# A two-layer sequence kernel on one core: output product and slot values in three rounded products of high and low parts

## Chip, cores and metric

One core of a Trainium2 chip. The metric is the device time of one execution in microseconds (us); lower is better. TensorE is called PE in rows, its weight loads PEld; VectorE is DVE, ScalarE ACT, GpSimd POOL.

## What is computed

Input x is 32 sequences of 512 tokens of 256 numbers, all float32. Two layers follow one another, each on a normalized x and added to x.

```
# layer 1, per sequence: attention by a kernel of random features
q     = tanh(x @ W_charge.T + b_charge)                  # one number per token
shell = normalize(x @ W_shell.T + b_shell)
phi   = (powers of q  (x)  [cos, sin](shell @ omega.T + rff_bias)) @ W_combine.T
attn  = softmax(causal(phi @ phi.T * decay / temp))
out   = (attn @ (x @ W_v.T + b_v)) @ W_out.T + b_out
# layer 2, per sequence: 64 slots, 8 chosen per token
h     = gelu([x, mean slot] @ w1.T + b1);  logits = (h @ w2.T + b2) / (|tau| + 0.1)
alpha = softmax over the 8 largest logits, 0 elsewhere   # tokens x 64
gi    = alpha.T @ x / sum of alpha                       # 64 x 256
S_new = gru(gi, slots)                                   # 64 x 256
slot_values = S_new @ wv.T + bv
out   = (alpha @ slot_values) @ wo.T + bo
```

The kernel folds wo into wv, so the last two lines are slot_values = S_new @ Wvo + bSV and out = alpha @ slot_values.

## The kernel before

The 32 sequences are worked in 16 pairs k = 0..15; d = 0, 1 is the sequence in the pair, b = 2k + d. Every engine has a queue written out by hand (an order of calls such as `values(n, 1); xm_t(f, 1, 0)`), with semaphores between them. The queue of each engine has an opening (pairs 0 to 4, to about 185 us), a loop `for it in range(3, 15)` that works on five pairs at once, and an end. In the loop p = it + 2 is the pair being normalized and projected, n = it + 1 the one in attention, f = it the one at the second layer's hidden product and routing, m = it - 1 the one in the GRU, g = it - 2 the one at its output. There are 8 banks of PSUM in three rings (T for transposes, L for logits, G for the rest); a step that takes a bank waits until the step that emptied its last user is done.

The steps that matter, by engine:
- TensorE: `xn_t` transposes the normalized x (line 332), `proj` multiplies it with high and low parts of the weights (349), `q_t`, `z_t` transpose the features, `phi` (392 to 398), `logits` (415), `e_t`, `values` (443), `xm_t`, `hidden` (476), `route` (488), `rt_t`, `gather` (511), `gi_t`, `gx_rz` and `gx_n` (526), `al_t` transposes alpha, `slot_v` (597) makes the slot values, `out_mm(k, u)` (621) the output of token blocks 2u and 2u + 1 of both sequences: sequence d lies in rows 64d to 64d + 63 of aT and SV.
- ScalarE: `ln_norm` (746) normalizes x with the scales of GpSimd, `xn_high` (756), `v_high` (768 to 771), `z_copy` (801) copies the feature transpose that the powers start from, `al_copy` (896), activations.
- VectorE: statistics, the low parts (`xn_low` 988, `v_low` 995, `probs_low` 1052, `xm_low` 1090), `row_max` (1044), `attended` (1068), `top` (1106, 1109), `chosen` (1134), `gathered` (1147), `gates`, `candidate`, `new_slots` (1182), `slot_values` (1190, adds the bias), `finish` (1199, adds the output to x).
- GpSimd: `ln_scale` (eight small operations that end at 1485), `lm_scale`, `lm_norm` (268), `slot_change` (294), `rnorm`, `phase`, `power(p, i)` (241: four products 512 wide, the first waits for z_copy), `shift8` (277), `alpha` (287).

Most large products are made as three float32r products of high and low parts: ScalarE rounds the operand to float32r (the high part), VectorE subtracts it from the original (the low part), and TensorE adds high x high, high x low and low x high. `slot_v` and `out_mm` are plain float32 products, which TensorE runs as two instructions each.

The loop of GpSimd before:

```python
for it in range(3, 15):
    p, f, m = it + 2, it, it - 1
    ln_scale(p, 0); ln_scale(p, 1); lm_scale(f, 0); lm_scale(f, 1); lm_norm(f, 0); lm_norm(f, 1)
    slot_change(m); rnorm(p); phase(p); power(p, 0); shift8(f, 0); power(p, 1); power(p, 2)
    shift8(f, 1); alpha(f, 0); power(p, 3); alpha(f, 1)
```

## Time and profile before

| | |
|---|---|
| median of 3 runs | 692.98 us (691.63 to 694.11) |
| profiled execution, its time | 692.77 us |
| its span, first to last instruction | 691.0 us |
| busy: PE, DVE, ACT, POOL | 97%, 88%, 74%, 56% |
| granted clock of TensorE, mean | 0.998 of full speed |

Busy time is the time in which an engine has an instruction in flight. Matmuls overlap, so a busy PE may still stand between two starts; the starts in the timeline show that. A group of instructions is given by its line, its output and inputs and its shape.

### The profile page before, as it was taken

The page shows a single profiled execution, that of the slowest core. Times are in us where ns is not written, and L with a number is a line of the kernel's source. Part 1 is how long each engine was busy: PE and PEld are TensorE (multiplying, and loading weights), DVE is VectorE, ACT ScalarE, POOL GpSimd, SP SyncE. Part 2 cuts the span into 40 slices and gives each one's busy share as a digit, 9 for nine tenths or more (in the row PEclk, how much of TensorE's full clock was granted, in tenths as well). Part 3 has the DMA queues.
Part 4 walks back from the last instruction along what each step waited for, and adds up shares of the span by engine and source line. Part 5 has one row for each costly group of instructions (what it writes and reads, how often), then busy time and mean ns, then how long its engine had stood idle before and what let it go on. Part 6 is the DMA issues. An engine that isn't in the chain of part 4 may idle for free.

```text
span 691.0 us, 15834 instructions
## 1 busy us (share of the span) xinstructions
PE 672.0 (97%) x4622; PEld 541.1 (78%) x4622; DVE 604.9 (88%) x2001; ACT 514.7 (74%) x1477; POOL 384.9 (56%) x818
## 2 busy tenths in 40 slices
...
GB/s 237 108 153 83 10 63 1 63 2 137 48 121 64 40 144 3 129 56 123 62 64 122 1 139 46 123 62 88 98 1 158 28 123 62 63 62 63 1 2 182
DMA packets 49115, 54.11 MB, mean 78 GB/s; under 512 B 6212, under 2 KB 40582, under 8 KB 49030
## 3 DMA queue, kind: packets, MB, share of 16 engines
...
q8 instruction: 38, 0.62, 0.4%
...
## 4 chain that ended last, share of the span: by engine, by line
PE 83%; issue 4%; DVE 3%; POOL 3%; SPq 3%; ACT 2%; DMA 1%; POOLq 0%; DVEq 0%; ACTq 0%
PE ps L321 17%; PE ps L349 16%; PE ps L443 15%; PE ps L476 6%; PE ps L415 6%; PE ps L526 6%; PE ps L511 4%; PE ps L621 4%; PE ps L488 2%; SPq L1635 2%; PE ps L392 2%; PE ps L398 2%; PE ps L597 2%; PE ps L395 2%; POOL xm L268 1%
## 5 line engine op out<-in xcount | busy, mean ns | idle before, releaser
L241 POOL TENSOR_TENSOR Z<-Z,QB 128x512 f32<-128x512 f32 x60 | 77.3, 1288 | 81.5 <-ACT Z L801 79.8
L746 ACT ACTIVATE xn<-X,rs 128x255 f32<-128x255 f32 x128 | 66.4, 599 | 72.0 <-POOL rs L1485 72.0
L443 PE MATMUL ps<-Vh,Eh 128*128 128x256 f32 x320 | 88.5, 304 | 0.1
L349 PE MATMUL ps<-W1h,xh 128*128 128x354 f32 x256 | 88.5, 346 | 0.0
L349 PE MATMUL ps<-W1h,xl 128*128 128x354 f32 x256 | 83.2, 325 | 0.6 <-DVE xl L988 0.5
L349 PE MATMUL ps<-W1l,xh 128*128 128x354 f32 x256 | 83.0, 324 | 0.0
L443 PE MATMUL ps<-Vl,Eh 128*128 128x256 f32 x320 | 80.8, 280 | 0.0
L995 DVE TENSOR_TENSOR Vl<-ps,Vh 128x256 fp32r<-128x256 f32 x128 | 53.5, 420 | 22.7 <-ACT Vh L771 20.2
L1052 DVE TENSOR_TENSOR El<-ps,Eh 128x128 fp32r<-128x128 f32 (+3 forms) x128 | 61.7, 483 | 13.3 <-ACT Eh L822 11.7
L812 ACT ACTIVATE E<-ps,nmax 128x128 f32<-128x128 f32 (+3 forms) x128 | 67.9, 536 | 5.2 <-DVE nmax L1044 4.9
L268 POOL TENSOR_SCALAR xm<-X,rs 128x256 f32<-128x256 f32 x120 | 67.6, 579 | 1.5 <-PE ps L511 0.8
L822 ACT ACTIVATE Eh<-ps 128x128 fp32r<-128x128 f32 (+3 forms) x128 | 55.4, 444 | 11.6 <-PE ps L321 9.2
L443 PEld LDWEIGHTS ps<-Vh,Eh 128*128 128x128 f32 x320 | 60.3, 188 | 4.5 <-DVE X L1068 3.0
L1044 DVE CUSTOM_DVE_ANT_0 ps<-ps,causal 128x128 f32<-128x128 f32 (+3 forms) x128 | 60.9, 498 | 2.7 <-PE ps L415 2.6
L443 PEld LDWEIGHTS ps<-Vl,Eh 128*128 128x128 f32 x320 | 60.4, 189 | 0.1
L1068 DVE SCALAR_TENSOR_TENSOR X<-ps,rinv,X 128x256 f32<-128x256 f32 x128 | 59.3, 474 | 1.1 <-PE ps L443 0.6
L443 PE MATMUL ps<-Vh,El 128*128 128x256 f32 x320 | 58.6, 280 | 0.7 <-DVE El L1052 0.7
L321 PE MATMUL ps<-ident,E 128*128 128x128 f32 x320 | 55.2, 278 | 0.9 <-DVE El L1052 0.4
L1079 DVE BATCH_NORM_STATS2 stats<-X 128x6 f32<-128x256 f32 x128 | 51.7, 415 | 0.0
L321 PEld LDWEIGHTS ps<-ident,E 128*128 128x128 f32 x320 | 36.4, 140 | 19.3 <-issue 13.2
L771 ACT ACTIVATE Vh<-ps 128x256 fp32r<-128x256 f32 x128 | 51.4, 401 | 0.0
L1090 DVE TENSOR_TENSOR xmL<-ps,xmT 128x512 fp32r<-128x512 f32 x62 | 42.4, 686 | 10.1 <-ACT xmT L833 9.6
...
## 6 DMA issues: line engine op xcount, KB each, us to landing
...
```

The source lines that it names most:

```text
L241: e.tensor_tensor(Z[:, i + 1, :], Z[:, i, :], QB[:, :], ALU.mult).then_inc(s["zm"], 1)
L268: ins = e.tensor_scalar(xm[:, b % 3, t, 0:D], X[:, b % NX, t, :], rs2[:, d, 2, t:t + 1], rs2[:, d, 1, t:t + 1], ALU.add, ALU.mult)
L321: ins = e.transpose(p[0:m, j * 128:j * 128 + 128], block_in, ident[:, :])
L349: ins = e.matmul(p[:, 0:FEATS], x[:, d, c, t * 128:t * 128 + 128], w[:, c, :], start=j == 0, stop=j == 5)
L443: ins = e.matmul(p[:, 0:D], w[:, r % 2, j * 128:j * 128 + 128], v[:, (2 * k + d) % 4, j, :], start=z == 0, stop=z == len(parts) - 1)
L746: ins = e.activation(xn[:, d, t, 0:D - 1], X[:, b % NX, t, 0:D - 1], ACT.Identity, bias=rs[:, d, 2, t:t + 1], scale=rs[:, d, 1, t:t + 1])
L812: e.activation(E[:, r % 3, 0:w], at["lg", r], ACT.Exp, bias=nmax[:, r % 8:r % 8 + 1], scale=-1.0, accum_out=rsum[:, r % 8:r % 8 + 1]).then ...
L822: e.activation(Eh[:, r % 2, 0:w], at["E", r][:, 0:w], ACT.Copy).then_inc(s["eh"], 1)
L995: e.tensor_tensor(Vl[:, b % 4, t, :], at["vs", b, t][:, 0:D], Vh[:, b % 4, t, :].bitcast(FP), ALU.subtract).then_inc(s["vl"], 1)
L1044: e.tensor_tensor_reduce(at["lg", r], at["lg", r], causal[:, N - w:N], 1.0, 3e38, ALU.add, ALU.min, nmax[:, r % 8:r % 8 + 1]).then_inc(s[" ...
L1052: e.tensor_tensor(El[:, r % 2, 0:w], at["E", r][:, 0:w], Eh[:, r % 2, 0:w].bitcast(FP), ALU.subtract).then_inc(s["ET"], 1)
L1068: e.scalar_tensor_tensor(X[:, b % NX, i, :], at["av", r][:, 0:D], rinv[:, r % 8:r % 8 + 1], X[:, b % NX, i, :], ALU.mult, ALU.add).then_in ...
```

## The change

`slot_v` and `out_mm` become three rounded products of high and low parts. `out_mm` stays as it was for pairs 0 and 15 (`EXACT`). ScalarE makes the high parts (`sn_high`, `sv_high`, `al_high`), GpSimd the low parts (`sn_low`, `sv_low`, `al_low`). The new parts lie in buffers of the first layer: those of the slots and of the slot values in xh, that of alpha in xl, alpha's transpose in hT; GIN and GI move into gt and gn. So steps that write those buffers get waits. The order of all four compute queues is new. Wvo is stored as Wvh and Wvl by two more VectorE operations in the setup. The core of the diff:

```diff
+        GIN = gt[:, :, :, :].rearrange("p c b s -> p (c b s)")
+        GI = gn
+        SNh = xh[:, 0, 0, 0:D].rearrange("p (c b s) -> p c b s", c=2, b=2)
+        SNl = xh[:, 0, 0, D:2 * D].rearrange("p (c b s) -> p c b s", c=2, b=2)
+        SVh = xh[:, 1, 1, 0:D]
+        SVl = xh[:, 1, 1, D:2 * D]
+        aTl = xl[:, 1, 1, :]
+        aTx = hT[:, 1, :]
+        EXACT = (0, NP - 1)
+        def projected(k, d):
+            return 8 * min(k + (3 if k else 4), NP - 1) + 4 * d + 4
 # slot_v
-                for c in range(2):
-                    if c == 0 and k == NP - 1:
-                        e.wait_ge(s["sh"], 1)
-                    else:
-                        e.wait_ge(s["sn"], k + 1)
-                    ins = e.matmul(p[:, 0:D], SN[:, c, :, :].rearrange("p b s -> p (b s)"), Wvo[:, c, :],
-                                   start=c == 0, stop=c == 1)
+                e.wait_ge(s["snh"], k + 1)
+                parts = [(SNh, w, c) for c in range(2) for w in (Wvh, Wvl)] + [(SNl, Wvh, c) for c in range(2)]
+                for j, (x, w, c) in enumerate(parts):
+                    if j == 4:
+                        e.wait_ge(s["snl"], k + 1)
+                    ins = e.matmul(p[:, 0:D], x[:, c, :, :].rearrange("p b s -> p (b s)"), w[:, c, :],
+                                   start=j == 0, stop=j == 5)
 # out_mm
-                    e.wait_ge(s["aT"], k + 1)
-                    e.wait_ge(s["sv"], k + 1)
+                    e.wait_ge(s["aT" if exact else "ath"], k + 1 if exact else k)
+                    e.wait_ge(s["sv" if exact else "svh"], k + 1 if exact else k)
+                parts = [(aTx, SV)] if exact else [(aT, SVh), (aTl, SVh), (aT, SVl)]
                 for t in range(2):
                     tok = slice((2 * u + t) * 128, (2 * u + t) * 128 + 128)
-                    for d in range(2):
+                    for j, (w, v) in enumerate(parts):
+                        if u == 0 and t == 0 and j:
+                            e.wait_ge(s["atl" if j == 1 else "svl"], k)
+                        for d in range(2):
...
+                            ins = e.matmul(p[:, t * D:t * D + D], w[own(d), tok], v[own(d), :],
+                                           start=j == 0 and not final, stop=j == len(parts) - 1,
+                                           skip_group_check=True)
 # ScalarE: waits of xn_high and gelu, new steps
+                if k >= 5 and c == d:
+                    e.wait_ge(s["of_mm"] if c else s["sv_mm"], 4 * (k - 4) + 4 if c else k - 3)
+                if k >= 3 and d == 1:
+                    e.wait_ge(s["atl"], k - 2)
+            def al_high(k):
...
+                e.wait_ge(s["aT"], k + 1)
+                if k > 1:
+                    e.wait_ge(s["of_mm"], 4 * k)
+                e.activation(aT[:, :], aTx, ACT.Copy).then_inc(s["ath"], 1)
+            def sn_high(k):
+                e.wait_ge(s["vs_mm"], projected(k, 0))
+                if k < NP - 1:
+                    e.wait_ge(s["sn"], k + 1)
+                    e.activation(SNh, SN[:, :, :, :], ACT.Copy).then_inc(s["snh"], 1)
...
+            def sv_high(k):
...
+                e.wait_ge(s["sv"], k + 1)
+                e.wait_ge(s["vs_mm"], projected(k, 1))
+                e.wait_ge(s["of_mm"], 4 * k)
+                e.activation(SVh, SV[:, :], ACT.Copy).then_inc(s["svh"], 1)
 # VectorE: new_slots waits for snl in place of sv_mm; gathered for sn; xn_low(p, 1, 1) for out_mm
-                    e.wait_ge(s["sv_mm"], k)
+                    e.wait_ge(s["snl"], k)
+            def end_low_setup():
+                e.wait_ge(s["snh"], NP)
+                e.tensor_tensor(SNl, SN[:, :, :, :], SNh.bitcast(FP), ALU.subtract).then_inc(s["snl"], 1)
 # GpSimd
+            def sn_low(k):
+                e.wait_ge(s["snh"], k + 1)
+                e.tensor_tensor(SNl, SN[:, :, :, :], SNh.bitcast(FP), ALU.subtract).then_inc(s["snl"], 1)
+            def al_low(k):
...
+                e.wait_ge(s["ath"], k)
+                e.wait_ge(s["vs_mm"], projected(k, 1))
...
+                e.tensor_tensor(aTl, aTx, aT[:, :].bitcast(FP), ALU.subtract).then_inc(s["atl"], 1)
+            def sv_low(k):
...
+                e.wait_ge(s["svh"], k)
+                e.tensor_tensor(SVl, SV[:, :], SVh.bitcast(FP), ALU.subtract).then_inc(s["svl"], 1)
```

The loops of TensorE (its changed lines), ScalarE and GpSimd:

```diff
 # TensorE
-                proj(p, 0, 2); e_t(n, 1); gx_n(m); xn_t(p, 1, 1); values(n, 0); proj(p, 0, 3); logits(n, 1)
-                out_mm(g, 1); xm_t(f, 0, 0); xm_t(f, 0, 1); e_t(n, 2); proj(p, 1, 0); proj(p, 1, 1)
+                xn_t(p, 1, 1); out_mm(g, 1); logits(n, 1); gx_n(m); e_t(n, 1); values(n, 0); proj(p, 0, 2)
+                proj(p, 0, 3); xm_t(f, 0, 0); proj(p, 1, 0); proj(p, 1, 1); xm_t(f, 0, 1); e_t(n, 2)
...
-                values(n, 3); z_t(p); rt_t(f); values(n, 4); values(n, 5); al_t(m); e_t(n, 6); slot_v(m)
+                values(n, 3); z_t(p); rt_t(f); values(n, 4); values(n, 5); slot_v(m); e_t(n, 6); al_t(m)
                 e_t(n, 7); values(n, 6); values(n, 7); phi(p); gather(f); logits(p, 0); out_mm(m, 0); gi_t(f)
 # ScalarE
+                sv_high(g); ln_norm(p, 0); gi_copy(m); xn_high(p, 0, 0); xn_high(p, 0, 1); expo(n, 0)
+                ln_norm(p, 1); v_high(p, 0, 0); expo(n, 1); expo(n, 2); expo(n, 3); v_high(p, 0, 1)
+                rz_tanh(m); probs_t(n, 0); xn_high(p, 1, 0); xn_high(p, 1, 1); v_high(p, 0, 2); probs_t(n, 1)
...
+                xm_copy(f, 1, 0); gelu(f, 0); xm_copy(f, 1, 1); sn_high(m); probs_t(n, 3); charge(p)
+                probs_t(n, 4); gelu(f, 1); sine(p); q_copy(p); rt_out(f); probs_t(n, 5); z_copy(p); expo(n, 6)
+                expo(n, 7); route_exp(f, 0); probs_t(n, 6); al_copy(m); probs_t(n, 7); route_exp(f, 1)
+                al_high(m)
 # GpSimd
+                ln_scale(p, 0); sv_low(g); ln_scale(p, 1); lm_scale(f, 0); lm_scale(f, 1); lm_norm(f, 0)
+                lm_norm(f, 1); slot_change(m); rnorm(p); phase(p); power(p, 0); sn_low(m); shift8(f, 0)
+                power(p, 1); power(p, 2); shift8(f, 1); power(p, 3); alpha(f, 0); al_low(m); alpha(f, 1)
```

In the opening, VectorE had `top(2, 0, 0); top(2, 0, 1); top(2, 1, 0); top(2, 1, 1); shift(2, 0); probs_low(3, 5); shift(2, 1); new_slots(1); attended(3, 3)`; now it has `top(2, 0, 0); top(2, 0, 1); attended(3, 3); shift(2, 0); new_slots(1)`. In the end the last pair's variance and normalization (`end_scale_a_setup`, `end_norm_a_setup`) stand earlier on VectorE, and `sn_high(15)` and `end_low_setup` come between the last slots and `slot_v(15)`.

## Rows read from the trace of the kernel before

**Rows 1.** The page, parts 1 and 4: busy time, and the chain by engine.

```profile
PE 672.0 (97%) x4622; PEld 541.1 (78%) x4622; DVE 604.9 (88%) x2001; ACT 514.7 (74%) x1477; POOL 384.9 (56%) x818
PE 83%; issue 4%; DVE 3%; POOL 3%; SPq 3%; ACT 2%; DMA 1%; POOLq 0%; DVEq 0%; ACTq 0%
```

**Rows 2.** Busy time by stage: stretch, us, then PE, PEld, DVE, ACT, POOL, clock, DMA.

```profile
60.00:185.00 125.00, 121.10 (x834) 96.35 (x833) 108.34 (x354) 98.45 (x275) 76.77 (x150) 1.00 0.22 56
305.70:345.50 39.80, 39.79 (x282) 32.64 (x282) 36.42 (x121) 31.27 (x91) 24.39 (x51) 1.00 0.29 80
...
650.00:691.00 41.00, 32.12 (x216) 23.87 (x214) 29.07 (x104) 12.99 (x25) 3.38 (x4) 0.97 0.24 78
```

**Rows 3.** Timeline of ScalarE, 300 to 345: start, us, what, [idle before, released by].

```profile
303.48 2.07 ACT L746 ACTIVATE xn<-X,rs 128x255 f32<-128x255 f32 x4 [5.87 <-POOL rs L1485]
...
331.15 0.59 ACT L801 ACTIVATE Z<-ps 128x512 f32<-128x512 f32 x1
...
343.32 2.07 ACT L746 ACTIVATE xn<-X,rs 128x255 f32<-128x255 f32 x4 [5.86 <-POOL rs L1485]
```

**Rows 4.** Timeline of PE, 304.2 to 306.7, the seam of a pass.

```profile
304.28 1.03 PE L621 MATMUL ps<-SV,aT 64*128 64x256 f32 x8
305.24 0.44 PE L321 MATMUL ps<-ident,GIN 128*128 128x128 f32 x2
305.70 1.06 PE L321 MATMUL ps<-ident,xn 128*128 128x128 f32 x8
306.60 0.28 PE L526 MATMUL ps<-GI,wih 128*128 128x128 f32 x1
```

**Rows 5.** Waits, whole kernel: us in total, times, longest.

```profile
ACT xn L746 <- POOL rs L1485: 72.0, 13, 8.0
```

**Rows 6.** Starts inside 304.275 to 304.290 (matmuls, loads) and 304.49 to 304.51 (loads).

```profile
304.28 0.38 PE L621 MATMUL ps<-SV,aT 64*128 64x256 f32 x2
304.28 0.19 PEld L621 LDWEIGHTS ps<-SV,aT 64*128 64x128 f32 x2
304.50 0.19 PEld L621 LDWEIGHTS ps<-SV,aT 64*128 64x128 f32 x2
```

**Rows 7.** Timeline of PE, 331.5 to 339.1: slot_v, and rounded matmuls of values.

```profile
334.44 1.03 PE L597 MATMUL ps<-Wvo,SN 128*128 128x256 f32 x4
335.31 0.60 PE L321 MATMUL ps<-ident,E 128*128 128x128 f32 x4
...
337.42 0.28 PE L443 MATMUL ps<-Vh,Eh 128*128 128x256 f32 x1
...
338.36 0.62 PE L443 MATMUL ps<-Vh,El 128*128 128x256 f32 x4
```

**Rows 8.** The page, part 5: a rounding copy of 256 columns.

```profile
L771 ACT ACTIVATE Vh<-ps 128x256 fp32r<-128x256 f32 x128 | 51.4, 401 | 0.0
```

**Rows 9.** Groups of instructions of POOL by shape: busy, mean ns | idle before.

```profile
L241 POOL TENSOR_TENSOR Z<-Z,QB 128x512 f32<-128x512 f32 x60 | 77.3, 1288 | 81.5 <-ACT Z L801 79.8
...
L287 POOL TENSOR_TENSOR AL<-lg,asum 128x256 f32<-128x256 f32 x30 | 18.4, 614 | 25.6 <-DVE asum L1127 10.4 <-issue 9.1 <-DVE lg L1134 6.2
...
L294 POOL TENSOR_TENSOR gt<-S,gn 128x256 f32<-128x256 f32 x15 | 11.0, 734 | 22.1 <-ACT gn L877 22.1
```

**Rows 10.** Timeline of POOL, 300 to 345, from the first power on.

```profile
331.82 1.29 POOL L241 TENSOR_TENSOR Z<-Z,QB 128x512 f32<-128x512 f32 x1 [6.07 <-ACT Z L801]
...
336.93 0.61 POOL L287 TENSOR_TENSOR AL<-lg,asum 128x256 f32<-128x256 f32 x1 [0.83 <-issue]
337.50 1.30 POOL L241 TENSOR_TENSOR Z<-Z,QB 128x512 f32<-128x512 f32 x1
339.55 0.61 POOL L287 TENSOR_TENSOR AL<-lg,asum 128x256 f32<-128x256 f32 x1 [0.76 <-DVE asum L1127]
```

**Rows 11.** Timeline of the end: PE's last slot_v, and DVE's slot_values.

```profile
682.58 1.03 PE L597 MATMUL ps<-Wvo,SN 128*128 128x256 f32 x4
683.64 0.42 DVE L1190 TENSOR_TENSOR SV<-ps,bSV 128x256 f32<-128x256 f32 x1 [0.19 <-PE ps L597]
```

**Rows 12.** Waits of PE in the opening, 60 to 185.

```profile
PE ps L597 <- DVE X L1068: 1.5, 1, 1.5
```

More of the change, by code:

```diff
@@ L168, in build @@
         SV = sb("SV", [128, D])
-        aT = sb("aT", [128, N])
+        aT = sb("aT", [128, N], FR)
         def stacked(d, j):
@@ L705, in _ @@
-            values(2, 4); hidden(1, 1); e_t(2, 5); z_t(3); logits(2, 2); route(1); gx_n(0); values(2, 5)
-            al_t(0); e_t(2, 6); rt_t(1); proj(4, 0, 0); values(2, 6); phi(3); xn_t(4, 1, 0); e_t(2, 7)
-            proj(4, 0, 1); proj(4, 0, 2); logits(3, 0); xn_t(4, 1, 1); values(2, 7); proj(4, 0, 3)
-            proj(4, 1, 0); e_t(3, 0); proj(4, 1, 1); proj(4, 1, 2); xm_t(2, 0, 0); e_t(3, 1); proj(4, 1, 3)
-            slot_v(0); values(3, 0); xm_t(2, 0, 1); logits(3, 1); out_mm(0, 0); e_t(3, 2); hidden(2, 0)
@@ L710, in _ @@
-            gather(1); out_mm(0, 1); e_t(3, 3); values(3, 1); gi_t(1); values(3, 2); xm_t(2, 1, 0)
-            xm_t(2, 1, 1); e_t(3, 4); gx_rz(1); q_t(4); hidden(2, 1); z_t(4); logits(3, 2); route(2); gx_n(1)
-            rt_t(2); values(3, 3); e_t(3, 5); al_t(1); values(3, 4); values(3, 5); e_t(3, 6); e_t(3, 7)
-            slot_v(1); values(3, 6); values(3, 7); phi(4); gather(2); logits(4, 0); out_mm(1, 0); gi_t(2)
+            proj(0, 0, 0); proj(0, 0, 1); xn_t(0, 1, 0); proj(0, 0, 2); proj(0, 0, 3); xn_t(0, 1, 1)
@@ new lines, in _ @@
+            proj(3, 1, 1); xm_t(1, 0, 1); e_t(2, 1); proj(3, 1, 2); proj(3, 1, 3); logits(2, 1); e_t(2, 2)
+            xn_t(4, 0, 0); values(2, 0); gather(0); logits(2, 2); q_t(3); e_t(2, 3); values(2, 1)
+            values(2, 2); hidden(1, 0); gi_t(0); xm_t(1, 1, 0); xm_t(1, 1, 1); values(2, 3); hidden(1, 1)
+            z_t(3); e_t(2, 4); xn_t(4, 0, 1); gx_rz(0); values(2, 4); e_t(2, 5); route(1); e_t(2, 6)
+            values(2, 5); al_t(0); rt_t(1); e_t(2, 7); values(2, 6); proj(4, 0, 0); phi(3); gx_n(0)
@@ new lines, in _ @@
+            proj(4, 0, 1); logits(3, 0); xn_t(4, 1, 0); proj(4, 0, 2); xn_t(4, 1, 1); proj(4, 0, 3)
+            values(2, 7); e_t(3, 0); proj(4, 1, 0); xm_t(2, 0, 0); e_t(3, 1); proj(4, 1, 1); proj(4, 1, 2)
+            xm_t(2, 0, 1); proj(4, 1, 3); hidden(2, 0); slot_v(0); e_t(3, 2); values(3, 0); logits(3, 1)
+            gather(1); out_mm(0, 0); logits(3, 2); q_t(4); gi_t(1); xm_t(2, 1, 0); values(3, 1); xm_t(2, 1, 1)
+            out_mm(0, 1); e_t(3, 3); gx_rz(1); e_t(3, 4); hidden(2, 1); values(3, 2); z_t(4); route(2)
```

380 lines of the change are left out of this document (203 added, 177 removed).

## Prediction

> **What bounds the kernel now.** First the page's busy shares and its chain of waits: TensorE is busy 97% of the span and carries 83% of the chain, so TensorE's work is the first candidate [rows 1]. Then the busy time by stage: in the loop of the schedule (here 305.7 to 345.5) TensorE is busy 39.79 of 39.80 us, VectorE 36.4, ScalarE 31.3, GpSimd 24.4; in the opening (60 to 185) TensorE leaves 3.9 of 125 us idle, and in the last 41 us it leaves 8.9 [rows 2]. The granted clock is 1.00 of full, the 2.4 GHz level, in loop and opening, and 0.97 in the last stretch.
>
> A busy share of 100% hides small waits, since a matmul's duration covers the pipeline. So I read the starts. One pass through the loop is 39.84 us (normalization of ScalarE at 303.48 and 343.32 [rows 3]). At the seam of a pass TensorE runs out_mm from 304.28, two transposes gi_t from 305.24, then eight xn_t from 305.70; the eight take 0.90 us to the next group, 0.11 each, so xn_t could have started near 305.46 and waited some 0.2 us [rows 4]. What it waits for is ln_norm on ScalarE, which itself stood idle 5.86 us for ln_scale on GpSimd [rows 3]; over the kernel ScalarE lost 72.0 us in 13 such waits [rows 5]. So there are two cycles of nearly one length: TensorE's own work, some 39.6 us, and the one through z_t, z_copy (331.15), four powers, two alphas and ln_scale on GpSimd, ln_norm (343.32), xn_t. The second is 0.2 us longer, and it is the one that ends last.
>
> **What the change does to TensorE.** out_mm: four calls with 64 rows, each split into two fp32 passes, 8 instructions. Two instructions, one for partitions 0 to 63 and one for 64 to 127, start inside one window of 15 ns, their weight loads too, and the next two loads start 0.22 us later [rows 6]: pairs run together, one each 0.22 us. Four pairs are 0.87 us; the 0.96 us up to gi_t [rows 4] hold the turn to full-height tiles as well. A rounded matmul of 256 columns takes one pass: eight from 337.42 to 338.36 are 0.1175 us each [rows 7]. Three products are six pairs, 6 x 0.118 = 0.71 us if pairs still run together. It saves 0.16 per call, 0.32 per pass (k = 1 to 14; pairs 0 and 15 stay fp32). slot_v: four fp32 instructions from 334.44 to 335.31, 0.87 us [rows 7]; six rounded ones are 0.71, saving 0.16. TensorE's own work falls by 0.48 us a pass, 39.6 to 39.1. No row shows rounded matmuls in 64-row pairs. The bounds are 0.71 (together) and 12 x 0.118 = 1.42 (one by one); I take 0.71, since the fp32 pairs are the nearest row [rows 6].
>
> **ScalarE** gets sn_high and sv_high (256 wide, 0.40 us each as v_high's third instruction [rows 8]) and al_high (512 wide, 0.59 as z_copy [rows 3]), 1.4 us a pass. al_high and sv_high fall into the 5.86 us in which it waits for GpSimd [rows 3], and cost nothing; behind sv_high's waits stands only ln_norm, which isn't ready. sn_high stands ahead of z_copy, but z_copy waits for z_t anyway, which stands behind values(n, 3) on TensorE; if that cover is gone it costs 0.4.
>
> **GpSimd** gets sn_low and sv_low (0.61 to 0.73 us, as the 256-wide subtraction and product there) and al_low (1.29, as a power) [rows 9]. This is where the change bites. Between z_copy (331.15) and ln_norm (343.32) lie 12.17 us [rows 3]. GpSimd's queue in them is power, shift8, power, power, shift8, alpha, power, alpha, ln_scale; it stood idle 0.83 us before the first alpha and 0.76 before the second, 1.59 together [rows 10]. Now sn_low stands behind the first power and al_low before the second alpha: 1.90 to 2.02 us. Operations behind one another start 0.04 early (alpha at 336.93 takes 0.61, the power starts at 337.50 [rows 10]), so the two add 1.82 to 1.94 and the idle time gives 1.59. The chain grows by 0.23 to 0.35; I take 0.25, since DVE's work before the alphas is hardly changed and both alphas are then ready. sv_low comes behind ln_scale(p, 0) and so isn't in it; it delays ln_scale(p, 1), whose transposes stand behind 28 gate and projection matmuls, over 3.3 us at 0.118. Behind al_low's wait for al_high stand alpha(f, 1), which gather needs, and ln_scale.
>
> The cycle through GpSimd also holds TensorE's work from xn_t to z_t, with one of the two out_mm calls in it, moved ahead of logits: -0.16. So a pass is 39.84 + 0.25 - 0.16 = 39.93, +0.1 us. TensorE alone would take 39.1 and waits 0.8 at xn_t; the wait that out_mm now has for sv_low (behind ln_scale, so ready about when ln_norm starts) falls into the same gap. Eleven passes load new rows (it = 3 to 13): +1.1 us. The bounds: if GpSimd's idle time took all of it, 39.68, -1.8 in all; with sn_low in z_copy's way, +0.5 a pass. The moved order makes TensorE's banks wait on other DVE steps (gx_n for v_low(p, 0, 1), proj(p, 0, 2) for finish(g, 1, 1)); between nothing and one 0.42 us DVE operation [rows 11]; I take nothing, as DVE has 3.4 us free per pass [rows 2]. The waits of xh and xl on slot_v and out_mm four pairs back, GIN and GI in gt and gn, and snl in place of sv_mm name work of the pass before or early in this one: nothing.
>
> **Opening.** Its 3.9 us of TensorE idle [rows 2] hold one wait of 1.5 us at slot_v(1) on an accumulation of DVE [rows 12]: the bank of slot_v(1) is freed by attended(3, 3), which stood behind all of top(2), shift(2) and new_slots(1). The new order has it behind the first half of top(2) only. I take half of the 3.9 back, -2.0; bounds 0 (new waits) and -3.9, +1 for two more 0.4 us subtractions in the setup.
>
> **End.** The last pass and the tail save TensorE 0.48 + 0.48, and the variance and normalization of pair 15 stand earlier on DVE. Against it the last slot_v starts at 682.58 and its sum at 683.64 [rows 11]; now sn_high (0.40) and end_low_setup (0.42) lie between the new slots and it, partly beside its first four matmuls. I take -0.8; bounds -2 and +1.
>
> **The sum**, against the profiled execution: span 691.0, its time 692.8, so 1.8 around it, 0.2 below the median of the three runs. 692.8 + 1.1 - 2.0 - 0.8 = **691.1 us**.
>
> **The rivals.**
> 1. TensorE's gain goes through (0.22). The 72 us row would have to be harmless: GpSimd's new work shorter than its idle time, or z_copy earlier. For it: TensorE is busy all through [rows 2] and the seam wait is only 0.2 us. Against it: the 1.59 us against 1.9. 11 x 0.48 = 5.3: 692.8 - 5.3 - 2.0 - 0.8 = 684.7; half of it 687.4.
> 2. Loads in line, or pairs one by one (0.07). A pair costs 0.22 as now, a call 1.30 instead of 0.87, a pass on TensorE 39.6 + 0.86 - 0.16 = 40.3, +0.46: 11 x 0.46 = 5.1, and with 1 us more in opening and end 696 to 697; one by one (1.42) 699. Against it: the loads of a pair start together [rows 6].
> 3. Slower, by the GpSimd chain (0.18): place, between the first power and ln_scale; price, sn_low and al_low at their upper rows, al_low waiting for al_high or power delayed by sn_high, 0.4 us more than taken; it decides from a chain that is 0.35 us longer than now on. +0.5 a pass: 692.8 + 5.5 - 2.8 = 695.5.
>
> **How the numbers follow.** Forecast 0.51, with its own range 688.5 to 694.0 (opening and end between their bounds, pass -0.05 to +0.25); rivals 0.22, 0.07, 0.18; 0.02 for anything else. 0.3% is 2.1 us, about what a measurement of this kernel tells from no change: faster is below 690.9, slower above 695.1. Faster: 0.22 and 0.22 of the forecast's 0.51, 0.44. Slower: 0.07, 0.12 of rival 3 and 0.03: 0.22. Within: 0.34. The range for 8 in 10 leaves out half of rival 1, the upper part of rival 3 and rival 2: 685.5 to 697.
>
> **What would show it.** Right: ln_norm in the loop still waits for GpSimd, passes of 39.8 to 40.1 us, TensorE's gap between gi_t and xn_t grown from 0.2 to about 0.8 us or moved to the third product of out_mm; no idle time of GpSimd before the alphas; twelve matmuls of out_mm in 0.7 us; slot_v in 0.7. Wrong: passes of 39.4 (rival 1), out_mm in 1.3 us (rival 2), gaps elsewhere in the pass (bank waits, not costed), a slot_v(1) that still waits.

## The result, and the profile after

The changed kernel took 704.16 us (703.18 to 705.54, 4 runs) against 692.92 for the kernel before on the same chip: a ratio of 1.0163 (95% interval 1.0146 to 1.018). The forecast was 691.1 with a range up to 697.0. The profiled execution has a span of 702.1 us, 11.1 more than before.

Where they lie, by the starts of z_copy on ScalarE (16 a kernel): the fifth, for pair 4, comes at 167.6 (166.4 before) and the sixth at 212.8 (211.6), so 1.2 us are lost ahead of the steady loop. The next ten passes take 40.59 each (39.82), 7.7 us in all. From the last z_copy to the end it is 83.4 us (81.2), 2.2 more. So it is above all the loop. Two passes of after, from z_copy to z_copy (busy us and instructions of each engine, granted clock):

```profile
293.97:334.55 40.58, 39.65 (x294) 32.75 (x293) 36.83 (x121) 31.89 (x95) 27.58 (x54) 1.00 0.29 79
334.55:375.13 40.58, 39.62 (x294) 32.69 (x293) 36.84 (x121) 31.92 (x95) 27.57 (x54) 1.00 0.29 79
```

TensorE was busy all but 0.01 us of a pass [rows 2]; now it idles 0.93. Its own work has become a little less, 39.64 for 39.79. So it waits. The page's chain of waits was 83% TensorE [rows 1]; now:

```profile
PE 63%; DVE 15%; POOL 9%; issue 6%; ACT 5%; DMA 1%; DVEq 0%; ACTq 0%; POOLq 0%; SPq 0%
```

TensorE's timeline of out_mm(g, 1) shows that the products run nearly as forecast: pairs together, twelve matmuls from 314.94 to 315.75. The first pair takes 0.22 us, the five behind it 0.12 each, 0.81 in all (0.96 before [rows 4], with the turn to full height behind it). slot_v takes six times 0.12, 0.72.

```profile
314.94 0.39 PE L638 MATMUL ps<-xh,aT 64*128 64x256 f32 x2
315.16 0.28 PE L638 MATMUL ps<-xh,xl 64*128 64x256 f32 x2
315.28 0.40 PE L638 MATMUL ps<-xh,aT 64*128 64x256 f32 x4
315.51 0.28 PE L638 MATMUL ps<-xh,xl 64*128 64x256 f32 x2
315.63 0.28 PE L638 MATMUL ps<-xh,aT 64*128 64x256 f32 x2
315.75 0.81 PE L427 MATMUL ps<-QK 64*128 64x384 f32 x4
```

At the seam of a pass TensorE waits three times (idle time before a row in brackets, with who ended it), for VectorE twice, for ScalarE's ln_norm once:

```profile
347.41 0.93 PE L427 MATMUL ps<-QK 64*128 64x128 f32 x8 [0.54 <-DVE QK L1097]
349.26 0.41 PE L333 MATMUL ps<-ident,gt 128*128 128x128 f32 x2 [0.20 <-DVE gt L1212]
349.84 0.30 PE L333 MATMUL ps<-ident,xn 128*128 128x128 f32 x1 [0.17 <-ACT xn L765]
```

Why VectorE is late stands in GpSimd's and VectorE's timelines of the same stretch (z_copy starts at 334.55). GpSimd:

```profile
335.22 1.29 POOL L253 TENSOR_TENSOR Z<-Z,QB 128x512 f32<-128x512 f32 x1 [5.67 <-ACT Z L822]
336.47 0.74 POOL L1620 TENSOR_TENSOR xh<-SN,xh 128x256 fp32r<-128x256 f32 x1
337.17 0.23 POOL L289 TENSOR_TENSOR m8s<-m 128x32 f32<-128x32 f32 x1
337.37 2.65 POOL L253 TENSOR_TENSOR Z<-Z,QB 128x512 f32<-128x512 f32 x2
339.97 0.43 POOL L289 TENSOR_TENSOR m8s<-m 128x32 f32<-128x32 f32 x1
340.36 1.29 POOL L253 TENSOR_TENSOR Z<-Z,QB 128x512 f32<-128x512 f32 x1
341.61 0.61 POOL L299 TENSOR_TENSOR AL<-lg,asum 128x256 f32<-128x256 f32 x1
342.19 1.27 POOL L1630 TENSOR_TENSOR xl<-hT,aT 128x512 fp32r<-128x512 f32 x1
343.87 0.61 POOL L299 TENSOR_TENSOR AL<-lg,asum 128x256 f32<-128x256 f32 x1 [0.42 <-issue]
```

VectorE:

```profile
339.76 0.54 DVE L1198 SCALAR_TENSOR_TENSOR lg<-lg 128x256 f32<-128x256 f32 x1
...
341.89 0.74 DVE L1043 BATCH_NORM_STATS2 stats<-X 128x6 f32<-128x256 f32 x2
342.56 1.19 DVE L1198 SCALAR_TENSOR_TENSOR lg<-lg 128x256 f32<-128x256 f32 x1
343.66 0.41 DVE L1043 BATCH_NORM_STATS2 stats<-X 128x6 f32<-128x256 f32 x1
```

The instruction at 342.56 is chosen(m, 1), which the second alpha waits for. It reads two SBUF tensors and takes 1.19 us; before, the same one took 0.41. It starts inside al_low (342.19 to 343.46) and ends 0.28 us behind it. The two statistics ahead of it, with one SBUF input each, take 0.74 together as ever, the second of them wholly inside al_low. And the other way round: GpSimd's small shift8 at 339.97, beside chosen(f, 0), takes 0.43 us and its like at 337.17 takes 0.23. So the theory at this point, the "shared port" of the expectations below, was: **an instruction of VectorE with two SBUF inputs and one of GpSimd that reads SBUF don't run side by side; the later is held until the earlier ends.** The rival: chosen is slow for a reason of its own, and the added work merely lengthens GpSimd's chain.

The Trainium skill states it as a rule ("SBUF — State Buffer", sections "SBUF: two separate sides" and "Who interferes with whom"): the two engines share a port pair, locked for a whole instruction, and a VectorE instruction with two SBUF inputs contends for it with a GpSimd instruction that reads SBUF. By that rule this trace agrees, with 1.19 against 0.41.

### The profile page after: what moved, and what is told of

The parts are those of the page before. It is cut to its first block, busy times and chain, and to the rows that moved or that the text cites. A ratio compares the mean times of both kernels' runs of the same rounds, so it can differ in the third digit from the quotient of the medians.

```text
span 702.1 us, 16306 instructions
## 1 busy us (share of the span) xinstructions
PE 669.8 (95%) x4766; PEld 540.0 (77%) x4766; DVE 610.4 (87%) x2004; ACT 523.9 (75%) x1520; POOL 428.4 (61%) x861
## 4 chain that ended last, share of the span: by engine, by line
PE 63%; DVE 15%; POOL 9%; issue 6%; ACT 5%; DMA 1%; DVEq 0%; ACTq 0%; POOLq 0%; SPq 0%
PE ps L361 17%; PE ps L333 13%; PE ps L455 6%; PE ps L488 6%; PE ps L538 6%; PE ps L427 4%; ACT xn L765 3%; DVE lg L1173 3%; DVE El L1115 2%; PE ps L500 2%; DVE m L1170 2%; PE ps L638 2%; POOL xl L1630 2%; DVE X L1131 2%; POOL rs L1556 2%
## 5 line engine op out<-in xcount | busy, mean ns | idle before, releaser
L361 PE MATMUL ps<-W1l,xh 128*128 128x354 f32 x256 | 82.7, 323 | 0.0
L843 ACT ACTIVATE Eh<-ps 128x128 fp32r<-128x128 f32 (+3 forms) x128 | 58.1, 455 | 6.9 <-PE ps L333 2.7
L333 PE MATMUL ps<-ident,E 128*128 128x128 f32 x320 | 57.3, 278 | 0.4 <-DVE lg L1182 0.4
L792 ACT ACTIVATE Vh<-ps 128x256 fp32r<-128x256 f32 x128 | 53.9, 421 | 0.0
L538 PEld LDWEIGHTS ps<-gn,wih 128*128 128x128 f32 x384 | 45.2, 192 | 9.3 <-DVE Vl L1058 6.0
```

Source lines behind the costliest of these rows:

```text
L333: ins = e.transpose(p[0:m, j * 128:j * 128 + 128], block_in, ident[:, :])
L361: ins = e.matmul(p[:, 0:FEATS], x[:, d, c, t * 128:t * 128 + 128], w[:, c, :], start=j == 0, stop=j == 5)
L538: ins = e.matmul(p[:, at_col:at_col + 128], wih[:, c, j * 128:j * 128 + 128], GI[:, c, :, :].rearrange("p b s -> p (b s)"), start=c == 0, ...
L843: e.activation(Eh[:, r % 2, 0:w], at["E", r][:, 0:w], ACT.Copy).then_inc(s["eh"], 1)
```

## The experiments

All times of this table are read from profiled executions. "Pass" is the mean of the ten passes from the sixth z_copy to the last; the next two columns and "held" are medians of steady passes. "To ln_norm" is from z_copy to the ln_norm behind it; "held" are the durations of chosen(f, 0) and chosen(m, 1), 0.41 undisturbed. The ratio is to the kernel before on the same chip.

| kernel | ratio (95%) | opening, to 6th z_copy | pass | to alpha(f, 1) | to ln_norm | held | behind last z_copy |
|---|---|---|---|---|---|---|---|
| before | 1 | 211.6 | 39.82 | 8.39 | 12.17 | 0.42, 0.41 | 81.2 |
| after | 1.0163 (1.0146–1.018) | 212.8 | 40.59 | 9.32 | 13.06 | 0.54, 1.18 | 83.4 |
| sn_early | 1.0166 (1.0146–1.0187) | 212.1 | 40.59 | 9.31 | 13.05 | 1.20, 0.41 | 84.2 |
| chosen_early | 1.0119 (1.0095–1.0143) | 212.5 | 40.30 | 9.08 | 12.78 | 0.53, 0.40 | 83.4 |
| al_late | 1.0176 (1.0144–1.0209) | 214.1 | 40.43 | 8.54 | 12.28 | 0.53, 0.41 | 86.4 |
| before_collide | 1.0135 (1.0112–1.0158) | 211.6 | 40.73 | 8.31 | 13.07 | 0.42, 1.30 | 82.0 |
| no_al_low | 1.0028 (1.0016–1.004) | 212.9 | 39.84 | 8.55 | 12.30 | 0.53, 0.41 | 83.7 |
| exact_out | 1.0063 (1.0039–1.0087) | 212.1 | 39.98 | 8.55 | 12.29 | 0.53, 0.41 | 84.4 |
| old_work_new_order | 1.015 (1.0132–1.0169) | 213.6 | 40.63 | 9.29 | 13.04 | 1.27, 0.41 | 83.4 |
| all_three | 1.0289 (1.0272–1.0306) | 216.0 | 41.22 | 8.29 | 13.08 | 1.20, 0.41 | 85.1 |
| al_split | 1.0091 (1.0077–1.0104) | 212.3 | 39.95 | 8.54 | 12.28 | 0.53, 0.41 | 84.2 |
| order_free | 1.0037 (1.0022–1.0051) | 212.3 | 39.76 | 8.43 | 12.16 | 0.41, 0.41 | 82.5 |
| before_new_ends | 1.0041 (1.0025–1.0057) | 214.0 | 39.82 | 8.40 | 12.16 | 0.42, 0.41 | 82.7 |
| new_work_old_loop | 1.0206 (1.0191–1.022) | 212.5 | 40.74 | 8.43 | 12.20 | 0.42, 0.41 | 85.1 |
| al_halves | 1.0148 (1.0127–1.0168) | 213.1 | 40.41 | 9.19 | 12.89 | 0.54, 0.63 | 85.2 |
| al_quarters | 1.0105 (1.0087–1.0124) | 211.9 | 40.12 | 8.53 | 12.28 | 0.53, 0.41 | 84.2 |
| slot_only | 1.0145 (1.0127–1.0162) | 217.5 | 39.96 | 8.51 | 12.28 | 0.53, 0.40 | 84.6 |

The two outer columns, and the ratio with them, also hold the granted clock. In the ten passes it is 1.00 in every run; outside them it isn't. Near 175 us it fell to its lower level (0.50 of full, 1.2 GHz) for 3.4 us in no_al_low, old_work_new_order and before_new_ends and for 6.8 us in al_late, all_three and slot_only. Behind the last z_copy, the last 3 us aside, it did so for 3.4 us in new_work_old_loop, al_halves and slot_only and twice in al_late. TensorE had stood idle for 0.9 and 1.7 us shortly before (up to 172.8 and 175.5 in before_new_ends), but it does so in order_free too, where no fall follows. The same stretch in these two, which have the same order up to the loop (columns as in [rows 2]):

```profile
176.20:179.60 3.40, 3.40 (x15) 2.93 (x13) 2.64 (x13) 1.27 (x4) 0.81 (x2) 0.50 0.04 13
```

```profile
176.20:179.60 3.40, 3.40 (x29) 3.22 (x27) 3.33 (x16) 1.62 (x4) 0.85 (x2) 1.00 0.02 7
```

15 matmuls in place of 29. It differs between executions of one kernel too: al_late took 702.7 us at a mean clock of 0.998 and 707.2 at 0.989. So the pass and the durations carry the argument, and small differences of the outer columns don't.

### Is chosen held by GpSimd?

**sn_early**, one swap in GpSimd's loop:

```
-  phase(p); power(p, 0); sn_low(m); shift8(f, 0)
+  phase(p); sn_low(m); power(p, 0); shift8(f, 0)
```

> The changed kernel with one swap in GpSimd's loop: the slots' low part (sn_low, 0.74 us) stands ahead of power(p,0), where GpSimd idles 5.67 us, instead of behind it. Everything behind it on GpSimd, al_low too, comes 0.70 us earlier after z_copy. Theory (shared port: VectorE's chosen(m,1), two SBUF inputs, is held back by al_low on GpSimd, 342.19 to 343.46, and so takes 1.19 us instead of 0.41): al_low then ends before or just as chosen(m,1) wants to start, chosen takes 0.4 to 0.5, alpha(f,1) comes 0.8 us earlier after z_copy, the pass falls from 40.59 to 39.8 and the time by about 8 us to 696. Rival (chosen(m,1) is slow by itself or waits for ScalarE; the added work only lengthens GpSimd's chain): chosen keeps its start and its 1.19 us, alpha(f,1) waits for it and comes no earlier, the pass stays at 40.5 to 40.6 and the time at 703 to 704.

chosen(m, 1) took 0.41 and yet nothing was gained: the pass stayed at 40.59. GpSimd's power(p, 3) now came earlier too, and chosen(f, 0) fell into it (GpSimd first, then VectorE):

```profile
338.76 1.31 POOL L253 TENSOR_TENSOR Z<-Z,QB 128x512 f32<-128x512 f32 x1
```

```profile
339.16 1.20 DVE L1198 SCALAR_TENSOR_TENSOR lg<-lg 128x256 f32<-128x256 f32 x1
```

The rival is out (an instruction slow by itself wouldn't be fast here and its twin slow), and so is my sum: the hold moved to the other chosen, and TensorE waits 0.7 us a pass for the attended behind it.

**chosen_early**, in VectorE's loop:

```
-  weight_sum(m, 1); slot_values(g); ln_stats(p, 0, 0); chosen(m, 1); ln_stats(p, 0, 1)
+  weight_sum(m, 1); chosen(m, 1); slot_values(g); ln_stats(p, 0, 0); ln_stats(p, 0, 1)
```

> The changed kernel with one move in VectorE's loop: chosen(m,1) stands right behind weight_sum(m,1), ahead of slot_values and ln_stats(p,0,0), so that it would start near 341.6 in place of 342.56, before al_low starts at 342.19. Shared port: it takes 0.41 us instead of 1.19, alpha(f,1) follows al_low at once (GpSimd's idle 0.42 us between them is gone), and VectorE is 0.8 us ahead from there on; the pass falls by 0.4 to 40.2, the time to about 700. Rival (slow by itself): chosen takes 1.19 us there too; alpha(f,1) still comes 0.4 earlier, but ln_stats behind it aren't earlier. The duration tells the two apart.

0.40 us, the pass 40.30, 0.1 short of the expected gain: started so early, chosen holds alpha(f, 0) on GpSimd, which took 0.83 us in place of 0.61:

```profile
340.45 0.83 POOL L299 TENSOR_TENSOR AL<-lg,asum 128x256 f32<-128x256 f32 x1
341.24 1.27 POOL L1630 TENSOR_TENSOR xl<-hT,aT 128x512 fp32r<-128x512 f32 x1
```

**al_late**: al_low leaves its place between the alphas for one behind the next ln_scale(p, 0).

```
-  power(p, 3); alpha(f, 0); al_low(m); alpha(f, 1)
+  power(p, 3); alpha(f, 0); alpha(f, 1)
-  ln_scale(p, 0); sv_low(g); ln_scale(p, 1)
+  ln_scale(p, 0); al_low(g); sv_low(g); ln_scale(p, 1)
```

> The changed kernel with al_low taken from between the two alphas and put behind the next ln_scale(p,0) on GpSimd; VectorE's order isn't touched. Shared port: nothing on GpSimd reads SBUF when chosen(m,1) starts at 342.56, it takes 0.41 us, alpha(f,1) starts near 343.0 instead of 343.87, ln_norm comes 0.87 us earlier after z_copy, the pass falls to 39.7 to 39.9, the time to 695 or 697. Rival (slow by itself): chosen ends at 343.74 as now, alpha(f,1) waits for it with 1.6 us of idle before it, and the pass stays at 40.6, though 1.27 us of work left the chain.

chosen took 0.41 and alpha(f, 1) came 0.78 us earlier, as the shared port has it, but the pass fell to 40.43 only, not to the 39.7 to 39.9 expected. A new wait took the place: out_mm(m, 0) stands for al_low and then for sv_low.

```profile
348.25 0.47 PE L638 MATMUL ps<-xh,aT 64*128 64x256 f32 x2
348.93 0.39 PE L638 MATMUL ps<-xh,xl 64*128 64x256 f32 x2 [0.22 <-POOL xl L1630]
349.62 0.50 PE L638 MATMUL ps<-xh,aT 64*128 64x256 f32 x4 [0.30 <-POOL xh L1637]
```

**before_collide**, the mirror, in the kernel before, VectorE's loop:

```
-  slot_values(g); ln_stats(p, 0, 0); chosen(m, 1); weight_sum(m, 1); ln_stats(p, 0, 1)
+  chosen(m, 1); weight_sum(m, 1); slot_values(g); ln_stats(p, 0, 0); ln_stats(p, 0, 1)
```

> The mirror, on the kernel before: chosen(m,1) is moved ahead of slot_values on VectorE, so that it starts near 337.8 in place of 338.76, inside GpSimd's power(p,3) (337.50 to 338.80, two SBUF operands), which it misses now. Shared port: chosen takes about 1.3 us instead of 0.41 and ends at 339.1, alpha(f,1) is about where it was, all behind it on VectorE is 0.9 us late, and the pass is 0 to 0.5 longer (time 693 to 698). Rival (no shared port between these two): 0.41 us, alpha(f,1) 0.7 us earlier, the pass at TensorE's 39.8, time 692 to 693.

This is the clearest run: not one instruction more than in the kernel before, and 9.5 us slower. GpSimd's power(p, 3) and VectorE's chosen(m, 1):

```profile
340.10 1.28 POOL L241 TENSOR_TENSOR Z<-Z,QB 128x512 f32<-128x512 f32 x1
```

```profile
340.38 1.29 DVE L1134 SCALAR_TENSOR_TENSOR lg<-lg 128x256 f32<-128x256 f32 x1
...
341.89 0.41 DVE L1190 TENSOR_TENSOR SV<-ps,bSV 128x256 f32<-128x256 f32 x1
```

I had the pass 0 to 0.5 longer; it was 0.91. alpha(f, 1) isn't late at all (8.31), but ln_stats is, ln_norm with it (13.07 for 12.17), and TensorE waits 0.76 us for slot_values, whose bank phi wants. The move itself puts slot_values behind chosen, but what stands ahead of ln_stats(p, 0, 1) is the same in both orders, so its delay is the hold. Here a hold of 0.89 us costs 0.91 a pass; old_work_new_order against order_free (below) has 0.86 and 0.87.

**al_halves**: al_low where the change has it, as two instructions of 256 columns.

```
+  h = slice(256 * u, 256 * u + 256)
-  e.tensor_tensor(aTl, aTx, aT[:, :].bitcast(FP), ALU.subtract)
+  e.tensor_tensor(aTl[:, h], aTx[:, h], aT[:, h].bitcast(FP), ALU.subtract)
```

> The changed kernel with al_low in its own place but as two instructions of 256 columns (about 0.65 us each). If VectorE is held until the GpSimd instruction that runs ends, and then gets its turn: chosen(m,1), which starts 8.0 us after z_copy, ends 0.3 us behind the first half and takes 0.5 to 0.7 us instead of 1.19; the second half waits for it; alpha(f,1) comes at most 0.2 earlier, VectorE's ln_stats and quarter products 0.5 to 0.6 earlier; pass 40.1 to 40.4, time 698 to 702. If VectorE is held as long as GpSimd has such work queued: 1.2 us as before, pass 40.6.

```profile
301.55 1.59 POOL L1633 TENSOR_TENSOR xl<-hT,aT 128x256 fp32r<-128x256 f32 x2
```

```profile
301.92 0.63 DVE L1200 SCALAR_TENSOR_TENSOR lg<-lg 128x256 f32<-128x256 f32 x1
```

0.63 us: held to the end of the first half (302.27) and 0.28 more. The second half starts at 302.23 and takes 0.91 for 0.72, held in its turn (1.59 for both). So a hold lasts for the one instruction that runs, and long instructions of GpSimd hold longest. The pass, 40.41, is at the upper end of what I expected.

### The new work or the new order?

**no_al_low**: al_low is left out, and with it the low part in the second product.

```
-  parts = ... [(aT, SVh), (aTl, SVh), (aT, SVl)]
+  parts = ... [(aT, SVh), (aT, SVh), (aT, SVl)]
```

> The changed kernel without al_low: the alphas' low part isn't made, and the output product's second product takes the high part once more, so TensorE's work is the same and the output is inexact. Shared port: nothing runs on GpSimd between the alphas, chosen(m,1) takes 0.41 us, alpha(f,1) starts 0.87 us earlier after z_copy, no second product waits for GpSimd (as it did when al_low was only moved); the pass falls from 40.59 to 39.4 to 39.7 and the time to 691 to 694. Rival (TensorE's own added loads and products set the pass): the pass stays above 40.2.

39.84 a pass, 0.75 less than after and 0.14 above the expected range: TensorE is busy 39.60 and waits 0.17 for ln_norm. al_low where it stands makes the loop's loss, by its work and its hold together; this run doesn't part the two.

**exact_out**: `EXACT = range(NP)`, the output product in fp32 in all passes.

> The changed kernel with the output product back in one fp32 product in all passes: al_high, al_low, sv_high and sv_low are gone, slot_v stays rounded (sn_high, sn_low stay), the order is the new one. Shared port: chosen(m,1) takes 0.41; GpSimd's chain is that of before and 0.70 for sn_low; TensorE has 0.32 a pass more than the changed kernel; the pass is 39.7 to 40.0, the time 693 to 696. Rival (the rounded slot values or the order cost as well): the pass stays above 40.2.

39.98, as the shared port has it; the time, 698.0, is 2 us above what I expected, since I had the opening and the end at before's length.

**old_work_new_order**: the kernel before, with the changed kernel's four orders and none of the six new steps.

> The kernel before with all four engines' orders of the changed kernel, opening and end too, and none of its six new steps. Theory: the loop's loss comes from the new work (al_low on the shared port) and not from the order: the pass is 39.8 to 39.9, chosen(m,1) takes 0.41. The opening's order is what makes z_copy(4) 1.2 to 1.4 us late, so this kernel has that too, and the time is 693 to 696. Rival (the order costs in the loop): pass above 40.2, time over 698. If z_copy(4) is where it was before (166.4 us), the opening's loss is the new work's.

Here I was plainly wrong: 40.63 a pass with no new work at all, and 1.015. The order alone costs as much as the change. The reason is again a hold, another one: GpSimd's loop has power(p, 3) ahead of alpha(f, 0), not behind it, and without sn_low that puts it under chosen(f, 0).

```profile
340.44 1.30 POOL L241 TENSOR_TENSOR Z<-Z,QB 128x512 f32<-128x512 f32 x1
```

```profile
340.75 1.27 DVE L1137 SCALAR_TENSOR_TENSOR lg<-lg 128x256 f32<-128x256 f32 x1
341.94 0.47 DVE L1071 SCALAR_TENSOR_TENSOR X<-ps,rinv,X 128x256 f32<-128x256 f32 x1
```

Behind chosen stands attended(n, 5), whose bank the values want: TensorE waits 0.7 us a pass for it.

```profile
PE ps L443 <- DVE X L1071: 2.2, 3, 0.7
```

**order_free** puts that to the test, one swap in the kernel of the last run:

```
-  shift8(f, 1); power(p, 3); alpha(f, 0); alpha(f, 1)
+  shift8(f, 1); alpha(f, 0); power(p, 3); alpha(f, 1)
```

> The old work in the new order took 40.63 a pass, with chosen(f,0) at 1.27 us under power(p,3). This is that kernel with one swap in GpSimd's loop: alpha(f,0) ahead of power(p,3), as in the kernel before, so that GpSimd waits idle while chosen(f,0) runs. Shared port: chosen(f,0) takes 0.41, TensorE's wait of 0.7 a pass for attended is gone, the pass is 39.8 to 40.0, the time 694 to 697. Rival (the new order costs by its other moves): the pass stays at 40.4 or more.

39.76: one swap of two GpSimd instructions gives 0.87 us a pass back, 8.7 in the ten passes. The new order by itself is even 0.06 a pass faster in the loop than the old one.

**all_three**: sn_low and chosen(m, 1) early and al_low late, together.

> The changed kernel with three moves: sn_low ahead of power(p,0), chosen(m,1) first on VectorE ahead of weight_sum(m,1), al_low behind ln_scale(p,0). Each of the first and the third alone gave nothing: sn_low early put chosen(f,0) under power(p,3) (1.20 us), al_low late made the output product wait 0.54 us for al_low and sv_low. Together: alpha(f,1) starts near z_copy + 8.0 us (9.3 in the changed kernel, 8.5 with al_low late alone), al_low ends 0.5 earlier than there and the output product waits 0 to 0.3; the pass is 39.6 to 39.9 and the time 693 to 696. If VectorE's chosen(f,0) under power(p,3) sets the pass, it is 40.2 or more.

41.22, the slowest: chosen(f, 0) under power(p, 3) as in sn_early, the wait for attended, and out_mm's waits for al_low and sv_low, 0.7 and 0.5 a pass. The last sentence of the expectation named the cause, not its size.

### Can the change pay, once nothing is held?

**al_split**: al_low in halves behind ln_scale(p, 0) and ln_scale(p, 1); out_mm(m, 0) reads only the first.

```
+  ln_scale(p, 0); al_low(g, 0); sv_low(g); ln_scale(p, 1); al_low(g, 1); lm_scale(f, 0)
```

> The changed kernel with al_low in two halves of 256 columns behind ln_scale(p,0) and behind ln_scale(p,1): the first half of the output product reads only the first. All six added steps are there, and nothing runs on GpSimd when VectorE's chosen(m,1) starts. Shared port: pass as without al_low, 39.8 to 39.9 (it was 39.85), time 693 to 696. Rival (al_low's own 1.27 us on GpSimd set the pass, wherever it stands): above 40.2.

39.95, 0.64 less than after with all of its work, and 0.05 above the expected range; the time, 698.8, is 2.8 above it. In the loop out_mm now waits for sv_low, up to 0.3 a pass.

**al_quarters**: pieces of 128, 128 and 256 columns, and alpha(f, 0) ahead of power(p, 3).

> The new work and order, al_low behind ln_scale(p,0) in pieces of 128, 128 and 256 columns with sv_low behind the first, and alpha(f,0) ahead of power(p,3). If what kept al_split at 39.95 was the output product's wait of 0.25 us for sv_low: that wait is 0 to 0.05 here and the pass is 39.6 to 39.75; with the new order's 2 to 3 us in the opening and behind the loop the time is 692 to 695. If GpSimd's chain binds all the same: 39.9 and 696 to 699.

Missed: 40.12, 0.17 more than al_split. A piece of 128 columns takes 0.46 us, not a quarter of 1.27, so sv_low comes only 0.25 earlier and the second piece is late. The starts of out_mm(m, 0) in al_quarters:

```profile
304.84 0.47 PE L640 MATMUL ps<-xh,aT 64*128 64x256 f32 x2
305.14 0.28 PE L640 MATMUL ps<-xh,xl 64*128 64x256 f32 x2
305.43 0.50 PE L640 MATMUL ps<-xh,aT 64*128 64x256 f32 x4
305.84 0.38 PE L640 MATMUL ps<-xh,xl 64*128 64x256 f32 x2
306.07 0.28 PE L640 MATMUL ps<-xh,aT 64*128 64x256 f32 x2
306.28 0.44 PE L333 MATMUL ps<-ident,gt 128*128 128x128 f32 x2
```

1.44 us; the same call takes 1.08 in no_al_low, where it waits for neither. But in al_split it takes 1.51, so this isn't what makes al_quarters the slower of the two. By the starts the 0.17 lie in the projections' matmuls `ps<-W1h,xh` (3.04 a pass for 2.87); what delays them no run shows.

**new_work_old_loop**: all of the new work, al_low split, sn_low ahead of power(p, 0), in the loop order of the kernel before.

> All of the new work in the loop order of the kernel before, with the six steps put where they meet no VectorE instruction of two SBUF inputs that something waits for: sn_low ahead of power(p,0), alpha(f,0) ahead of power(p,3), al_low in halves behind ln_scale(p,0) and ln_scale(p,1). TensorE's work is 0.34 a pass less than before by the no_al_low run (out product 0.2, slot values 0.14). Expected: chosen(f,0) and chosen(m,1) 0.41 each, pass 39.5 to 39.8, time 690 to 694; this would beat both kernels if TensorE's gain goes through. If VectorE's and GpSimd's way from the route to ln_norm binds as in the kernel before: 39.8 and 693 to 695.

Missed by 0.9: 40.74, though both chosen took 0.41 and ln_norm came at 12.20. TensorE waits 0.5 us a pass for xn_low (`PE ps L333 <- DVE xl L1052: 1.4, 3, 0.5`), which the change lets wait for out_mm(g, 1), since its buffer now holds the alphas' low part; in the old order out_mm(g, 1) stands behind logits(n, 1). And sn_low in its new place holds turns(p), a tensor_scalar with one SBUF input. GpSimd, then VectorE:

```profile
329.61 0.74 POOL L1621 TENSOR_TENSOR xh<-SN,xh 128x256 fp32r<-128x256 f32 x1 [0.25 <-ACT xh L943]
```

```profile
329.87 0.64 DVE L1070 TENSOR_SCALAR tg<-ang 128x256 f32<-128x256 f32 x1
```

Undisturbed it takes 0.28. So with the new buffers the old loop order loses, at least with these places for the six steps.

**slot_only**: the kernel before with rounded slot values alone.

> The kernel before, with its order, and of the new work only slot_v in three rounded products (sn_high behind xm_copy(f,1,1) on ScalarE, sn_low behind power(p,0) on GpSimd); the output product stays one fp32 product. TensorE's work is 0.14 us a pass less; GpSimd's 0.70 us goes into its idle 0.83 and 0.76 us ahead of the alphas. If TensorE sets the pass: 39.65 to 39.75, time 690.5 to 692. If VectorE's way to ln_norm sets it: 39.8 to 39.9, 692 to 694; a chosen held for more than 0.3 us would show as 40 or more.

Missed: a pass of 39.96, and 5.9 us lost in the opening, where my places for sn_high(0) and sn_high(1) were poor (TensorE waits there 3.2 us for ScalarE's E and 1.2 for sn_high) and the clock was at its lower level for 6.8 us, so of this run only the pass speaks. Eight of the ten passes take 39.87 to 39.95, the other two 40.17 and 40.19; in one of these chosen(m, 1) took 0.60. TensorE's gain of 0.14 doesn't appear: ln_norm comes 0.11 later than in the kernel before, behind a chosen(f, 0) of 0.53.

**before_new_ends**: the kernel before, its loop untouched, with the new order in the opening and behind the loop.

> The kernel before, its loop untouched, with the changed kernel's order in the opening (up to the loop) and behind it, on all four engines, without the new steps. The pass is 39.8. If the new order is what delays both ends: z_copy(4) at 166.5 to 167.6 (166.4 before), z_copy(5) at 212 to 213.6 (211.6), gather(14) to gather(15) 22.9 to 23.6 us (22.25), in all 1 to 3 us slower: 694 to 696. If the new work is: 693.

2.4 us more ahead of the loop and 1.5 behind it, with no new work. Of the 2.4 only 1.0 lie ahead of the fifth z_copy; behind it the clock falls for 3.4 us. order_free, with the same order up to the loop and no fall, loses 0.7 ahead of the sixth z_copy and 1.3 behind the last. So the order alone costs some 2 us outside the loop, not 3.9. Behind the loop gather(15) now waits for end_alpha, which VectorE has behind both chosen of pair 15; before, no such wait stands there.

```profile
676.61 1.76 PE L511 MATMUL ps<-xm,AL 128*64 128x257 f32 x13 [1.83 <-DVE AL L287]
```

The changed kernel has the same wait with 2.0 us. Its opening has waits for the copies of Z by DMA (1.7 us, 0.4 in the kernel before) and for ln_norm (1.0) ahead of the fifth z_copy, and for El (1.7) and Eh (0.9) behind it; I haven't separated them.

## Why the prediction was wrong, point by point

- **What bounds the kernel: right.** Two cycles of nearly one length, TensorE's and the one over GpSimd to ln_norm. In the kernels where out_mm and xn_low make TensorE wait for nothing new, the pass is the way from z_copy to ln_norm and 27.5 to 27.7 us, held or not: 12.16 and 39.76, 12.30 and 39.84, 12.78 and 40.30, 12.89 and 40.41, 13.06 and 40.59, 13.07 and 40.73.
- **TensorE's own gain: right in kind, too large.** Pairs do run together (rival 2 is out). slot_v gave 0.15 (0.16 forecast; its starts take 0.72 for 0.87), out_mm with the logits behind it 0.21 a pass (0.32; 4.28 for 4.49 in no_al_low): the first pair of a rounded call takes 0.22 or 0.30, not 0.12. TensorE's busy time fell by 0.15 in all, not 0.48. The order didn't take the rest: by the mean of ten passes TensorE is busy 39.81 us before, 39.68 in order_free (new order, old work) and 39.58 in no_al_low. Of the 0.35 that the two products give up between these two, their neighbours take 0.34 (`ps<-Vh,El` 2.65 a pass for 2.45, al_t 0.59 for 0.44, by the starts); why stays open.
- **GpSimd's chain: the step that failed, in two terms.** "I take 0.25, since DVE's work before the alphas is hardly changed and both alphas are then ready." In fact ln_norm came 0.89 us later (13.06 for 12.17), alpha(f, 1) 0.93. *First term, the added work:* al_low ended 8.9 us after z_copy, so alpha(f, 1) could have followed at 8.87, 0.48 behind the old 8.39. That is about the upper bound of 0.35 and 0.2 for shift8, held by chosen(f, 0); the idle 1.59 us [rows 10] was used up. *Second term, missing altogether:* alpha(f, 1) came at 9.32, since al_low held the chosen that it waits for: 0.45. The 0.42 us in which GpSimd stands idle before the second alpha are its mark; I had forecast none. I checked that VectorE's instructions hadn't changed in number and took their duration for fixed; duration was what al_low changed.
- **"out_mm in the cycle: -0.16":** the pass grew by 0.77 where ln_norm grew by 0.89, so about 0.12 of it came.
- **The moved order: "I take nothing".** It costs nothing by bank waits, but old_work_new_order shows 0.8 a pass by a hold that the swap of alpha(f, 0) and power(p, 3) makes when sn_low isn't there. In the changed kernel sn_low shifts power(p, 3) out of that place, and only the partial hold of 0.54 is left, under the end of power(p, 2).
- **Opening, -2.0 forecast, +1.2 measured; end, -0.8 forecast, +2.2 measured.** Both signs wrong. slot_v(1)'s wait of 1.5 us is gone, but the waits for El and Eh have come in its place: from the fifth z_copy to the sixth it is 45.2 us before and after, and the 1.2 are lost ahead of the fifth. I counted the one wait that the order removes and not those that a reordered stretch gets. In the end 0.8 of the 2.2 lie ahead of gather(14) and 1.4 between it and gather(15); before_new_ends, its loop untouched, has 0.9 and 0.7 there. So about 2 of these 3.4 us come by order alone, and the rest isn't separated.
- **Rival 3** had the right place and sign, +0.5 a pass, but another mechanism than the one that doubled it.
- **The sum:** 10 passes of 0.77, 1.2 and 2.2 make the 11.1 us; forecast were 1.1, -2.0 and -0.8. So of the 12.8 us between forecast and result 6.6 lie in the loop, 3.2 in the opening and 3.0 in the end; no rival came near either, the slowest stood at 699.

The hold could have been seen before the change. In the opening of the kernel before, new_slots runs under three powers, and its two instructions take 0.98 and 1.37 us, 0.42 in the loop:

```profile
172.50 4.10 POOL L241 TENSOR_TENSOR Z<-Z,QB 128x512 f32<-128x512 f32 x3
```

```profile
173.09 0.98 DVE L1177 SCALAR_TENSOR_TENSOR gt<-grz,gt 128x256 f32<-128x256 f32 x1
174.10 1.37 DVE L1182 SCALAR_TENSOR_TENSOR SN<-gt,gn 128x256 f32<-128x256 f32 x1
```

I read means by group, where 15 instructions hide one.

What stays open: which of its waits make the opening slower, where the rest of the end's loss comes from, and why TensorE's gain is taken back next to the new products. No version tried beats the kernel before; the nearest are no_al_low (inexact) and order_free, at 1.0028 and 1.0037.
